# The last samples of a convolution stage: where the next attention begins, and in what order DVE, POOL and TensorE end the stage

## What is computed

```
def bit_linear(x, w):      # rows of x rounded to 8 bits, w to -1, 0, 1
    scale = 127 / max(|x|) per row;  xq = round(x * scale) / scale
    return xq @ wq.T

# first feed-forward layer, on layernorm(x)
h = bit_linear(x, w1)                       # 256 -> 1024
h = silu(depthwise_conv1d(h, 3 taps) + b)   # along the rows of a sample
x = x + bit_linear(h, w2)                   # 1024 -> 256

# second attention, on layernorm(x), 16 heads of 16, keys and values from ctx (77 rows)
q = layernorm_of_each_head(z @ Wq.T) * g + b
k = layernorm_of_each_head(ctx @ Wk.T) * g + b
x = x + softmax(q k.T) v @ Wp.T + bp
```

## Time and profile before

| | |
|---|---|
| median of 3 runs | 1141.67 us (1141.02 to 1144.6) |
| the profiled execution, its own time | 1140.88 us |
| its span, first to last instruction | 1139.2 us |
| mean granted TensorE clock | 0.982 |
| busy: PE, DVE, ACT, POOL | 94%, 66%, 41%, 46% |
| convolution stage with its first and last borders | about 128 to 270 us of the span |

### The profile page before, as it was taken

The page is one execution under the profiler, slowest core; times in us unless marked ns, Lnnn a source line. Parts: engine busy times, 40 slices in busy tenths (PEclk is TensorE's granted clock), DMA queues, the critical chain, the costliest instruction groups (busy, mean ns, idle before and its releaser), DMA issues.

```text
span 1139.2 us, 22102 instructions
## 1 busy us (share of the span) xinstructions
PE 1075.2 (94%) x7985; PEld 878.0 (77%) x7985; DVE 746.9 (66%) x1697; ACT 468.0 (41%) x938; POOL 523.9 (46%) x512
## 2 busy tenths in 40 slices
PE   9999989978899999999989999999999999999997
PEld 5888756656778666998868999999998688875564
DVE  5799779978878447889842222222222999987784
ACT  2554677755565312121112222222222456653466
POOL 5645235576874223768765010000363757531352
PEclk9999999989999999999979999999999989999999
DMA  6999900002000300001147241311221200000001
GB/s 211 371 405 388 338 2 2 25 1 90 1 1 2 105 0 1 1 1 38 47 145 273 91 159 58 112 37 37 73 71 43 60 10 11 2 1 1 1 28 47
DMA packets 45129, 93.66 MB, mean 82 GB/s; under 512 B 3933, under 2 KB 19070, under 8 KB 42486
## 3 DMA queue, kind: packets, MB, share of 16 engines
q1 hardware_dynamic: 36646, 62.24, 15.4%
q0 software_dynamic: 7104, 29.14, 7.1%
q10 hardware_dynamic: 1296, 1.18, 0.3%
HBM read 39.02 MB, written 51.51 MB: 79 GB/s over the span
## 4 chain that ended last, share of the span: by engine, by line
PE 65%; DVE 15%; POOL 7%; issue 5%; ACT 4%; DMA 2%; POOLq 1%; PEldq 0%; DVEq 0%; SPq 0%; ACTq 0%; PEld 0%
PE PS L2500 10%; PE PS L2510 10%; PE PS L1109 7%; PE PS L2009 4%; PE PS L2365 3%; PE PS L1122 3%; PE PS L1087 3%; PE PS L1077 2%; PE PS L1725 2%; PE PS L2354 2%; PE PS L1888 2%; PE PS L1035 2%; POOL big L695 1%; DMA expert_out<-scr 1%; POOL expert_in L2278 1%
## 5 line engine op out<-in xcount | busy, mean ns | idle before, releaser
L2534 ACT ACTIVATE scr<-PS,W 128x128 f32<-128x128 f32 x148 | 53.5, 367 | 192.6 <-PE PS L2500 192.6
L2500 PEld LDWEIGHTS PS<-scr 128*128 128x128 f32 x992 | 116.4, 192 | 5.9 <-issue 2.4
L2500 PE MATMUL PS<-scr 128*128 128x128 f32 x992 | 118.6, 276 | 2.1 <-issue 1.5
L2510 PE MATMUL PS<-scr 128*128 128x256 f32 x496 | 112.2, 379 | 0.0
L2565 DVE TENSOR_SCALAR scr<-PS,W 128x128 f32<-128x128 f32 x148 | 51.2, 350 | 86.6 <-PE PS L2500 86.6
L727 POOL TENSOR_TENSOR scr<-scr,small 128x1232 f32<-128x1232 f32 x32 | 72.0, 2251 | 74.8 <-DVE small L478 74.7
L868 ACT ACTIVATE big<-PS 128x512 f32<-128x512 f32 x144 | 73.2, 523 | 70.4 <-PE PS L1087 69.9
L2510 PEld LDWEIGHTS PS<-scr 128*128 128x128 f32 x496 | 91.8, 190 | 11.2
L2571 DVE TENSOR_TENSOR scr<-PS,W 128x256 f32<-128x256 f32 x37 | 15.7, 425 | 128.8 <-PE PS L2510 119.4
L2611 POOL DMA_DIRECT2D expert_out<-scr x28 | 15.2, 545 | 160.6 <-DVE scr L2571 157.0
L1109 PEld LDWEIGHTS PS<-scr,big 128*128 128x128 f32 x640 | 81.5, 192 | 8.3 <-issue 5.1
(11 more groups left out here) (425 smaller groups left out, 2463.8 us busy)
## 6 DMA issues: line engine op xcount, KB each, us to landing
expert_in<-zeros SPq DMA_DIRECT2D x1, 19712.0 KB, 59.3
expert_out<-zeros SPq DMA_DIRECT2D x1, 19712.0 KB, 112.2
scr<-ew_in POOLq DMA_DIRECT2D x12, 1024.0 KB, 6.5
scr<-expert_in SPq DMA_DIRECT2D x38, 128.0 KB, 2.1
big<-ew_in POOLq DMA_DIRECT2D x4, 1024.0 KB, 9.2
expert_out<-scr POOLq DMA_DIRECT2D x28, 128.0 KB, 2.0
W<-pack SPq DMA_DIRECT2D x1, 2458.0 KB, 9.3
W<-pack SPq DMA_DIRECT2D x1, 2152.0 KB, 8.5
```

The source lines that it names most:

```text
L2500: ins = pe.matmul(bank(1 + f % 4, G), e_w1[slot][:, k, f * P:(f + 1) * P], e_xT[:, k, :], start=(k == 0), stop=(k == C - 1))
L2510: ins = pe.matmul(bank(5 + t, D), e_h[:, f, t * P:(t + 1) * P], e_w2[slot][:, f, :], start=(f == 0), stop=(f == FC - 1))
```

## The change

In iteration 6 (B - 2):

- DVE normalizes the rows of the attention's sample 0 (`sample_rows(v, 1, 0)`) between `hidden` and the first `half_largest`, no longer at the iteration's end. For this POOL makes `sample_rstd(0)` ahead of `rounded(5, 0)`, no longer behind it.
- DVE takes the statistics of sample 1 at the end of iteration 6, ahead of `key_vars(1)`, no longer at the start of iteration 7.
- PE transposes sample 0 ("z", 0) at the end of iteration 6, behind `hidden(7, 3)`.

In iteration 7 (B - 1) and behind it:

- DVE starts with `sample_rows(1)`, `sample_stats(2)` and `query_vars(0)`, and only then multiplies sample 6 (`scaled`). It then rounds the first half of sample 6 itself (new function `rounded` in `ffn0_dve`); POOL no longer does.
- DVE ends with `head_normed(0)`, `sample_rows(2)`, `key_vars(2)`, `second_added(6)`, `last_rounded(7)`; before, `key_vars(2)` and `second_added(6)` came first.
- PE makes the queries of sample 0 between `convolved(7, 1)` and `convolved(7, 2)`, in bank 1, and ("z", 1) behind the keys. `second_made(6)` comes behind `row2(7)`, before it came ahead of ("z", 1). Of 8 and 3 `clocked` matmuls 4 are left.
- ACT keeps ("z", 0) and ("q", 0) where PE makes them.
- POOL takes `key_rstd(1)` between the two `query_rstd`.
- The last scales use bank 6, the last keys bank 0, and the last convolution banks 5 and 6.

```diff
--- before.py
+++ after.py
@@ -381,7 +381,7 @@
                 ring[(lay_,) + key_] = len(ring)
 
         def ring_bank(lay, *key):
-            return 4 + ring[(lay,) + key] % 2
+            return 1 if (lay,) + key == (1, "q", 0) else 4 + ring[(lay,) + key] % 2
 
         def PTILE(lay, u):
             return NT * lay + u
@@ -988,7 +988,7 @@
             n = ring[(lay,) + key]
             if n >= 2:
                 pe.wait_ge(at_["ring_free"], n - 1)
-            return 4 + n % 2
+            return ring_bank(lay, *key)
 
         def extra_made(pe, lay, kind, j):
             s = at_
@@ -1479,13 +1479,13 @@
             else:
                 power(g, f_rstd[i % 2], f_ve[i % 2], f_mv[i % 2][:, :, 1]).then_inc(rstd_ready, 1)
 
-        ROW2 = [4] * (B - 1) + [0]
-        KV_BANK = [4] * (B - 1) + [6]
-        AMAX_BANK = 0
+        ROW2 = [4] * (B - 1) + [6]
+        KV_BANK = [4] * (B - 1) + [0]
+        AMAX_BANK = [0] * (B - 1) + [6]
 
         def conv_bank(i, p, r):
 
-            return (2, 3)[r] if p % 2 == 0 else (0, 1)[r] if (i, p) == (B - 1, PAIRS - 1) else (5, 6)[r]
+            return (2, 3)[r] if p % 2 == 0 else (5, 6)[r]
 
 
         def ffn0_dve(v, ch):
@@ -1522,12 +1522,20 @@
             def scales(i):
 
                 v.wait_ge(s["amaxT_psum"], i + 1)
-                ch.link(v.tensor_reduce(f_am2, bank(AMAX_BANK, T * P).rearrange("p (t n) -> p t n", t=T), AX.X, ALU.max))
+                ch.link(v.tensor_reduce(f_am2, bank(AMAX_BANK[i], T * P).rearrange("p (t n) -> p t n", t=T), AX.X, ALU.max))
                 ch.link(v.tensor_scalar(f_am2, f_am2, 1e-5, None, ALU.max))
                 ch.inc(v.tensor_scalar(f_deq2[i % 3], f_am2, f_mean127[:, 1:2], None, ALU.mult))
                 ch.link(v.reciprocal(f_sc2, f_am2))
                 v.tensor_scalar(f_sc2, f_sc2, 127.0, None, ALU.mult).then_inc(s["wide2_ready"], 1)
                 v.wait_ge(s["wide2_ready"], i + 1)
+
+            def rounded(i, n):
+
+                fs = slice(n * PAIRS, (n + 1) * PAIRS)
+                v.wait_ge(s["o_psum"], i)
+                v.wait_ge(s["scaled0_ready"], i + 1)
+                v.tensor_scalar(f_aq[:, fs, :], f_y[i % 2][:, fs, :], ROUND, ROUND, ALU.add,
+                                ALU.subtract).then_inc(s["aq0_ready"], 1)
 
             def last_rounded(i):
 
@@ -1549,17 +1557,21 @@
             for i in range(B):
                 if i + 2 < B:
                     ternary_stats(v, ch, i + 2)
+                elif i == B - 2:
+                    sample_stats(v, ch, 1, 0)
                 else:
-                    sample_stats(v, ch, 1, i + 2 - B)
+                    sample_rows(v, 1, 1)
+                    sample_stats(v, ch, 1, 2)
+                    query_vars(v, ch, 0)
                 if i:
                     scaled(i - 1, 0)
                     scaled(i - 1, 1)
                 if i == B - 1:
-                    sample_rows(v, 1, 1)
-                    sample_stats(v, ch, 1, 2)
-                    query_vars(v, ch, 0)
+                    rounded(i - 1, 0)
                 if i + 1 < B:
                     hidden(i + 1, (0, 1))
+                if i == B - 2:
+                    sample_rows(v, 1, 0)
                 half_largest(i, 0)
                 if i == B - 1:
                     second_added(v, i - 2)
@@ -1576,13 +1588,14 @@
                     quant_rounded(v, ch)
                 if 2 <= i < B - 1:
                     second_added(v, i - 2)
-                if i >= 5:
+                if i == B - 2:
+                    sample_stats(v, ch, 1, 1)
+                if 5 <= i < B - 1:
                     key_vars(v, ch, i - 5)
-                if i == B - 2:
-                    sample_rows(v, 1, 0)
-            second_added(v, B - 2)
             head_normed(v, 0)
             sample_rows(v, 1, 2)
+            key_vars(v, ch, 2)
+            second_added(v, B - 2)
             last_rounded(B - 1)
 
         def ffn0_pool(g):
@@ -1605,19 +1618,20 @@
             for i in range(B):
                 if i + 2 < B:
                     ternary_rstd(g, i + 2)
-                if i:
+                if i == B - 2:
+                    sample_rstd(g, 1, 0)
+                if 1 <= i < B - 1:
                     rounded(i - 1, 0)
                 if i == 1:
                     g.wait_ge(at_["o_full"], NT)
                 if 1 <= i <= 4:
                     second_zeroed(i - 1)
                 if i == B - 2:
-                    sample_rstd(g, 1, 0)
                     key_rstd(g, 0)
-                    key_rstd(g, 1)
             sample_rstd(g, 1, 1)
             sample_rstd(g, 1, 2)
             query_rstd(g, 0)
+            key_rstd(g, 1)
             query_rstd(g, 1)
 
         def ffn0_act(a):
@@ -1675,12 +1689,14 @@
             rows(1)
             for i in range(B):
                 silus(i, 0)
+                if i == B - 1:
+                    extra_kept(a, 1, "z", 0)
                 silus(i, 1)
+                if i == B - 1:
+                    extra_kept(a, 1, "q", 0)
                 if i:
                     row2(i - 1)
                 absolutes(i, 0)
-                if i == B - 1:
-                    extra_kept(a, 1, "z", 0)
                 silus(i, 2)
                 if i + 1 < B:
                     normed(i + 1)
@@ -1690,8 +1706,6 @@
                     rows(i + 2)
                 if i:
                     rounded(i - 1, 1)
-                if i == B - 1:
-                    extra_kept(a, 1, "q", 0)
                 if i < 4:
                     values_kept(a, 1, i, KV_BANK[i])
                 else:
@@ -1730,7 +1744,7 @@
             def largest(i):
                 pe.wait_ge(s["amax_ready"], i + 1)
                 for t in range(T):
-                    ins = pe.transpose(bank(AMAX_BANK, P, t * P), f_amax[:, t * P:(t + 1) * P], ident)
+                    ins = pe.transpose(bank(AMAX_BANK[i], P, t * P), f_amax[:, t * P:(t + 1) * P], ident)
                 ins.then_inc(s["amaxT_psum"], 1)
 
             def row2(i):
@@ -1761,21 +1775,21 @@
             convolved(0, 0)
             for i in range(B):
                 convolved(i, 1)
+                if i == B - 1:
+                    pe.wait_ge(s["g_ready"], PAIRS * B)
+                    extra_made(pe, 1, "q", 0)
                 convolved(i, 2)
+                if i == B - 1:
+                    pe.wait_ge(at_["ring_free"], ring[1, "z", 0] + 1)
                 if i:
                     row2(i - 1)
                 convolved(i, 3)
-                if i == B - 1:
-                    pe.wait_ge(s["row2_ready"], i)
-                    extra_made(pe, 1, "z", 0)
                 if i + 1 < B:
                     normed(i + 1)
                 if i >= 2:
                     if i == 2:
                         pe.wait_ge(s["w_ready"], C + 4 + 1)
                     second_made(pe, i - 2)
-                if i == B - 1:
-                    extra_made(pe, 1, "q", 0)
                 if i + 1 < B:
                     for p in range(PAIRS - 1):
                         hidden(i + 1, p)
@@ -1783,17 +1797,19 @@
                 if i + 1 < B:
                     convolved(i + 1, 0)
                 else:
-                    pe.wait_ge(s["silu_ready"], PAIRS * i + PAIRS - 1)
-                    clocked(pe, 2, 8)
+                    extra_made(pe, 1, "z", 1)
+                    pe.wait_ge(s["silu_ready"], PAIRS * B - 1)
+                    clocked(pe, 2, 4)
                 largest(i)
                 if i + 1 < B:
                     hidden(i + 1, PAIRS - 1)
-            second_made(pe, B - 2)
-            extra_made(pe, 1, "z", 1)
-            clocked(pe, 2, 3)
+                if i == B - 2:
+                    pe.wait_ge(at_["ksq_ready"], i - 4 + 1)
+                    extra_made(pe, 1, "z", 0)
             pe.wait_ge(at_["ksq_ready"], 4)
             extra_made(pe, 1, "q", 1)
             row2(B - 1)
+            second_made(pe, B - 2)
             extra_made(pe, 1, "kt", 0)
             extra_made(pe, 1, "qt", 0)
```

## The result

| | before | after |
|---|---|---|
| median of 4 executions, us | 1141.83 (1141.02 to 1144.6) | 1132.72 (1130.92 to 1135.14) |
| ratio, 95% interval | | 0.9928 (0.9912 to 0.9945) |
| profiled execution: time, span | 1140.88, 1139.2 | 1130.92, 1129.2 |
| mean granted clock | 0.982 | 0.992 |

The two medians lie 9.1 us apart. The ratio, which is the figure with an interval, means 8.2 us less, with 6.3 to 10.0 as its interval. The direction, the place and the mechanism came out as forecast.

A forecast was written before the change was run, and what follows sets the result against it. DVE was taken as the bound, idle 8.91 us in five gaps. 230.36 + 21.41 work + 2.16 gaps, less 0.26 overlap, put `last_rounded` at 253.67, 6.4 us earlier: 1141.67 - 6.4 = 1135.3 us, range 1133.9 to 1138.9.

The forecast's parts named there:

- The bound and the cause: DVE bounds; its 4.59 us gap comes from POOL's rounding ahead of the root, its 1.23 us gap from PE's clock.
- Work on DVE: From 230.36 to `last_rounded`, 20.80 us of DVE work stays and the new rounding adds 0.61: 21.41 us.
- Gap at `sample_rows(0)`: DVE's `sample_rows(0)` is held for the first 0.9 us of POOL's rounding of sample 5: a new wait of 0.50 us.
- The first rival: POOL's rounding of sample 5 holds `sample_rows(0)` to its end: gap 3.1 in place of 0.50 us, time 1137.9; 17%.
- (a): DVE's gap behind `largest(6)`, for the way over PE: 0.53 us.
- (c): DVE's gap behind `largest(7)`: again 0.53 us.
- (b): DVE's gap at `sample_rows(1)`, waiting for POOL's root with `key_vars(1)` beside it: 0.31 us.
- (d): DVE's gap at `second_added(6)`, waiting for PE's `second_made(6)`: 0.29 us with the hop.
- (e): DVE's gap at `last_rounded`: 0, as the scales on ACT are ready by about 251.7 and DVE is later.
- The second rival: PE's clock falls after all in its idle 1.4 us before `largest(7)`: gain 3.2 to 4.8 us, time 1137.7; 15%.
- the sum: `last_rounded` starts at 253.67 in place of 260.07, and this 6.4 us carries over whole: 1140.88 becomes 1134.5 us.
- gap 0: Low end of the forecast's range, 1133.9 us: no wait at `sample_rows(0)` in place of 0.50 us.

The follow-up runs named there:

- before_dve_round: Kernel before, with only the rounding of sample 6's first half moved from POOL to DVE: 1139.2 us, ratio 0.9982.
- before_filled: Kernel before, with 30 in place of 8 unread matmuls on PE ahead of the last sample's transposes: 1139.54 us, ratio 0.9983.
- after_rows_later: Changed kernel with `sample_rows(v, 1, 0)` moved behind `hidden(i + 1, (2,))`, into the end of POOL's rounding: 1132.24 us, one execution.
- after_unfilled: Changed kernel without its 4 unread matmuls ahead of `largest(7)`: 1132.94 us beside 1139.09 of before, ratio 0.9951.
- after_delayed: Changed kernel with 40 in place of 4 unread matmuls ahead of `largest(7)`: 1138.85 us beside 1138.72 of before, ratio 0.9999.
- after_look: Changed kernel, unedited, run for one more trace: 1139.56 us, one execution.
- after_pool_round: Changed kernel with the rounding of sample 6's first half given back to POOL, behind the roots: 1138.87 us beside 1139.09, ratio 0.9999.

## Why the mechanism came as forecast, and which step of the forecast failed

**The bound and the cause: right.** The 4.59 us gap came from the rounding on POOL ahead of the root, and the 1.23 us gap from PE's clock: `before_dve_round` closes the one and `before_filled` the other.

**Work on DVE.** 21.41 us with 0.26 of overlap given back, 21.15, was forecast. Measured: 23.06 less three gaps (1.39) and the hold (0.22), 21.45. So the forecast was 0.30 too low. Part of that is overlap that did not come back, behind two of the closed gaps. `second_added(6)` starts at 250.17, 0.06 behind the end of L666, and L1547 at 251.08, 0.03 behind the end of `second_added(6)`. The two `scaled` took 2.41 us in place of 2.33.

**Gap at `sample_rows(0)`: the kind of hold right, its size off.** The pair took 0.95 us in place of 0.73, so 0.22 and not 0.50. POOL's two small operations ended at 227.46, 0.56 ahead of DVE, where I had 0.41. The first L423 took 0.63 us and its twin 0.40, so it was held until about 228.25, 0.8 us behind POOL's start, where I had 0.9. The first rival, a hold to POOL's end, fell: the rounding went on until 231.10, and DVE ran four more instructions whole under it at their usual times, the second L423 among them. The Trainium skill ("SBUF — State Buffer", the section on the two separate sides) has whichever engine starts first hold the shared ports for its whole instruction, against a DVE instruction with two SBUF inputs or in a mode that uses both ports; by that the wait would have been 3.1 us. It was 0.22, so the rule doesn't hold for L423 under this rounding.

It does hold for the same L423 under other instructions of POOL. The prediction said that no row shows such an instruction under this rounding, and took 126.96 alone for the rival. It passed over rows of L423 itself, in the trace of the kernel before, first DVE, then POOL:

```profile
54.73 2.31 DVE L423 TENSOR_SCALAR scr<-X,small 128x256 f32<-128x256 f32 x2
```

```profile
54.31 2.24 POOL L727 TENSOR_TENSOR scr<-scr,small 128x1232 f32<-128x1232 f32 x1 [2.10 <-DVE small L478]
```

The pair took 2.31 us, its first 1.98 until 56.71, 0.15 behind POOL's end. So the rival was better founded than the prediction had it, and 0.22 us was owed to what POOL was doing: its rounding lets DVE in between. Under the rounding L423 was held when it started 0.56 behind POOL's start (by 0.23 us) and again when it started 2.72 behind it (by 0.67 us, to 0.15 behind POOL's end, in `after_rows_later`), and not at 1.11. Instructions with two SBUF inputs were held at its start alone. In the new kernel L1519 took its usual 0.68 at 230.69, 0.4 us ahead of the rounding's end, and in the old one at 2.71 us behind the start of the rounding at 216.19:

```profile
218.90 0.68 DVE L1519 TENSOR_TENSOR scr<-scr 128x512 f32<-128x512 f32 x1
```

Why the two kinds differ was not tested.

**Other gaps.** (a) 0.53 and (c) 0.53 as forecast; (b) 0.33 against 0.31; (d) 0.06 against 0.29, and counted with the work above; (e) none, as forecast. All terms together: 6.65 against 6.4, and the start of `last_rounded` is 0.25 us earlier than forecast.

**PE's clock.** The second rival didn't happen: 1.22 us idle, full clock at 246 to 250. In `after_unfilled`, with 2.17 us idle, it is 0.70 at 247 to 250, and the loss of 1.71 us is that rival's lower price, 1.6.

**The step that failed is the sum**, as it was put: "Behind this point both are the same program, so 1140.88 becomes 1134.5", taken with a range whose low end was only "gap 0". The sum carried one local distance over to the whole time and gave the other 1110 us no width of their own. The two are the same program behind that point, as far as `after_delayed` can tell, and a carry-over in the mean is consistent with the runs: 6.65 us lie within each of the three intervals (6.3 to 10.0; 5.2 to 10.6; 5.0 to 8.9 us). What does not hold is that single executions, and so medians of three or four, are the same there. Low stretches of PE's clock near 129, 282, 920 and 1035 us come and go in traces of either kernel, each worth from 0.5 us up to the 6.7 of after_look (the one at 577 is in every trace). The chips differ too: medians of before were 1141.2 and 1139.1 on two of them, and 1138.4 and 1138.7 in two sessions on a third. The base of the forecast, 1141.67 from three executions, is slower than all of these, by 0.5 to 3.3 us, and the forecast's range had room for 1.4 below its centre. With the local gain that the runs confirm, 1141.83 - 6.65 is 1135.2; the median lies 2.5 below it, and the first profiled execution shows where such an amount comes from: 1.6 at 125 to 140, before the change begins, and 1.7 at 925 to 940. That these stretches fall by chance is shown for the two kernels by their coming and going in traces of one program, and for `after_pool_round` it is not. What decides it in one execution was not found. So on which side of the range's edge the median of four executions fell was partly chance.

**Left open.** The three comparisons give 8.2, 7.9 and 6.9 us, all above 6.65. Each interval holds 6.65, and a lasting remainder of about 1 us is neither shown nor excluded. One rival for it was not tested: that the new kernel has the low stretch near 920 less often than the old one (it is in one of its four traces, and in two of the old kernel's four; of the eight single traces of edited kernels other than `after_pool_round` none has it, six of new ones and two of old ones). At 575 to 640 the traces of after are 0.5 to 1.1 us shorter than the first of before, but other traces of before differ by up to 0.25 there and two experiments by 0.7 and -1.4, so I draw nothing from it.

## What to carry to other kernels

When a long operation stands in one engine's queue between a short result and its user, change the order and the engine together, and follow each dependency of the new order: either alone uncovers the next wait (the engine alone 1.5 us here, the order alone 3.8, both 6.65). Fillers that keep PE busy through a wait are worth their place as long as the path runs through PE behind it: in one trace, four of them are worth 1.7 us here. Compare a change of half a per cent by a distance between two instructions within each trace, and give the forecast of the whole time the width of the base's own executions, which on this kernel is more than the whole list of small local doubts.

## What the runs showed of the hardware

A POOL rounding of 128x1024 numbers (3.64 us) does not hold DVE off throughout. The tensor-with-scalar L423 took 0.63 us when it started 0.56 behind POOL's start, its twin 0.40 directly behind that, and 1.07 us when it started 0.92 ahead of POOL's end. An instruction with two SBUF inputs took 1.56 in place of 0.68 us at the rounding's start, and 0.68 from 1.05 us behind it on, near the end too. A POOL subtraction of 128x1232 numbers (L727, 2.24 us) held L423 to its own end: 1.98 us in place of 0.40. A POOL power on 128x2 numbers took 1.59 us beside DVE's long multiplication and 0.72 us beside none. PE's granted clock is not a property of the program alone: the same 16 us of the same kernel ran at 0.50 in one execution, with 64 matmuls, and at 1.00 in another, with 151, and that alone was worth 6.7 us of 1138.
